# Value and gate projections in 512-column chunks through the two halves of `ogbuf`

## What is computed

```
mod = (silu(c) @ wmod) -> sa, ca, ga, sb, cb, gb
h = layernorm(x) * (1 + ca) + sa
q, k, v = h @ Wq.T, h @ Wk.T, h @ Wv.T          # 1024, 1024, 2048 wide; 4 heads
g = log_sigmoid(h @ Wgk1.T @ Wgk2.T + bgk2) / 32
o = gated linear attention(q, k, v, g)          # a recurrence over tokens
o = o * rsqrt(mean(o * o) + eps) * rms_w
x = x + ga * ((o * silu(h @ Wg.T)) @ Wout.T)    # gate 2048 wide
h = layernorm(x) * (1 + cb) + sb
x = x + gb * moe(h)                             # 8 experts, d_ffn 2048, top 2
```

## Time and profile before

| what | value |
|---|---|
| median of 3 runs | 3640.89 us |
| the profiled execution, its own time | 3633.7 us |
| its span on the slowest core (core 0) | 3632.2 us |
| spans of the 8 cores | 3603.2 to 3632.2 us |
| TensorE busy, share of the span | 2730.2 us, 75% |
| VectorE, ScalarE, GpSimd busy | 26%, 22%, 7% |
| share of the chain that ended last: TensorE, DMA | 64%, 9% |

### The profile page before, as it was taken

One profiled execution on the slowest core, in us unless ns is written; L12 is line 12 of the kernel. 1 busy time (PEld: TensorE's weight loads), 2 busy tenths in 40 slices (PEclk: granted clock), 3 DMA queues, 4 the chain that ended last, 5 costly groups with the idle time before them and its releaser, 6 DMA issues.

```text
span 3632.2 us, 37091 instructions; the slowest of 8 cores (3603.2 to 3632.2 us)
## 1 busy us (share of the span) xinstructions
PE 2730.2 (75%) x12923; PEld 1256.0 (35%) x12923; DVE 928.5 (26%) x1769; ACT 812.4 (22%) x1458; POOL 267.2 (7%) x463
## 2 busy tenths in 40 slices
PE   1474566467645755559999999999559999999997
PEld 0152225123411531114444444444124444444443
DVE  0323232333233223422112111212431111221221
ACT  0314231423342234211221112111321022111210
POOL 0010001001000100000100000000000010001000
PEclk9985678577757865669999999999679999999998
DMA  9361235034303520213543454434033344345334
GB/s 209 60 102 21 36 60 90 1 46 73 67 0 47 96 44 7 38 24 70 88 68 61 70 87 70 68 63 79 6 52 57 71 81 71 63 70 89 64 65 138
DMA packets 84362, 233.49 MB, mean 64 GB/s; under 512 B 7851, under 2 KB 8236, under 8 KB 82006
## 3 DMA queue, kind: packets, MB, share of 16 engines
q0 software_dynamic: 82400, 214.09, 35.4%
q1 hardware_dynamic: 1782, 17.03, 1.3%
HBM read 436.76 MB, written 8.39 MB: 123 GB/s over the span
## 4 chain that ended last, share of the span: by engine, by line
PE 64%; ACT 10%; DVE 9%; DMA 9%; issue 6%; DVEq 0%; ACTq 0%; POOL 0%; POOLq 0%
PE p L833 25%; PE p L804 22%; PE p L550 7%; PE p L675 3%; DMA vslab<-w1t 3%; DMA bigbuf<-wmod 3%; PE p L470 3%; DVE S L659 2%; ACT S_bf L663 2%; DMA ogbuf<-WgTt 1%; DMA ogbuf<-WvTt 1%; ACT bigbuf L606 1%; ACT scratch L629 1%; ACT scratch L621 1%; DVE scratch L451 1%
## 5 line engine op out<-in xcount | busy, mean ns | idle before, releaser
L804 PE MATMUL p<-hbuf,vslab 128*128 128x512 bf16 x4096 | 900.7, 381 | 19.9 <-DMA vslab<-w1t 14.5
L811 ACT ACTIVATE bigbuf<-p 128x512 bf16<-128x512 f32 x512 | 306.2, 598 | 1442.1 <-PE p L804 1401.8
L804 PEld LDWEIGHTS p<-hbuf,vslab 128*128 128x128 bf16 x4096 | 400.7, 98 | 515.6 <-issue 51.7
L833 PE MATMUL p<-bigbuf,wvg 128*128 128x512 bf16 x2048 | 460.6, 387 | 35.5 <-DVE bigbuf L816 35.5
L833 PE MATMUL p<-bigbuf,gslab 128*128 128x512 bf16 x2048 | 447.2, 379 | 0.0
L842 DVE SCALAR_TENSOR_TENSOR xTsb<-p,modc,xTsb 128x512 f32<-128x512 f32 x256 | 180.4, 746 | 743.8 <-PE p L833 743.8
L816 DVE TENSOR_TENSOR bigbuf<-bigbuf,vslab 128x1024 bf16<-128x1024 bf16 x256 | 177.3, 692 | 702.7 <-ACT bigbuf L811 701.0
L833 PEld LDWEIGHTS p<-bigbuf,wvg 128*128 128x128 bf16 x2048 | 202.6, 99 | 290.9 <-issue 60.6
L833 PEld LDWEIGHTS p<-bigbuf,gslab 128*128 128x128 bf16 x2048 | 200.4, 98 | 241.6
L550 PE MATMUL p<-ogbuf,hbuf 128*128 128x256 bf16 x1024 | 148.2, 315 | 111.0 <-DMA ogbuf<-WgTt 58.2
L794 POOL DMA_DIRECT2D vslab<-w1t x128 | 90.4, 708 | 1295.6 <-PE p L804 1253.6
(11 more groups left out here) (133 smaller groups left out, 1694.6 us busy)
## 6 DMA issues: line engine op xcount, KB each, us to landing
vslab<-w1t POOLq DMA_DIRECT2D x128, 512.0 KB, 6.3
wvg<-w2t POOLq DMA_DIRECT2D x64, 512.0 KB, 7.0
gslab<-w2t POOLq DMA_DIRECT2D x64, 512.0 KB, 9.1
hbuf<-WoutTt POOLq DMA_DIRECT2D x51, 256.0 KB, 5.2
bigbuf<-wmod POOLq DMA_DIRECT2D x8, 1536.0 KB, 16.7
wvg<-WvTt POOLq DMA_DIRECT2D x16, 512.0 KB, 9.2
ogbuf<-WvTt POOLq DMA_DIRECT2D x16, 512.0 KB, 5.7
wvg<-WgTt POOLq DMA_DIRECT2D x16, 512.0 KB, 9.5
```

What stands on the lines that cost most here:

```text
L804: T(lambda e, k=k, n2=n2, mi=mi, wb=wb, pbk=pbk: e.matmul(pbk[:, :], wb[:, mi * 1024 + k * 128: mi * 1024 + (k + 1) * 128], hbuf[:, k * 10 ...
L811: C(lambda e, m=m, n2=n2, pbk=pbk: e.activation(out=bigbuf[:, m * 1024 + n2 * 512: m * 1024 + (n2 + 1) * 512], in_=pbk[:, :], func=AF.Gelu ...
L833: T(lambda e, k=k, n2=n2, wb=wb, pbk=pbk: e.matmul(pbk[:, :], wb[:, k * 128:(k + 1) * 128], bigbuf[:, k * 1024 + n2 * 512: k * 1024 + n2 * ...
```

## The change

The chunks become 512 columns wide, 4 of `Wv` and 4 of `Wg` a slab. The pool of four is no longer used in this stage: chunk `nv` goes to half `nv % 2` of `ogbuf`, both halves under the one `Buf` `bogf`, and each chunk is loaded by two DMAs, which put their 256 columns beside each other in each of the 8 k-tiles. Matmuls, copies, Silu and products become 512 wide and half as many.

```diff
-            wvg_pool[0] = [wvg[:, 0:2048], wvg[:, 2048:4096],
-                           ogbuf[:, 0:2048], ogbuf[:, 2048:4096]]
-            bwvg_pool[0] = [bwvg[0], bwvg[1], bogf, bogf]
+            vg_bufs = [ogbuf[:, 0:4096], ogbuf[:, 4096:8192]]
...
-                for nv in range(8):
-                    wb, wbb = stream_wvg_chunk(wdram_, nv, 8, 256)
+                for nv in range(4):
+                    wb = vg_bufs[nv % 2]
+                    wbb = bogf
+                    for c_ in range(2):
+                        G(lambda e, nv=nv, c_=c_, wb=wb, wdram_=wdram_: e.dma_start(
+                            out=wb.rearrange("p (kt cm) -> p kt cm", kt=8)
+                            [:, :, c_ * 256:(c_ + 1) * 256],
+                            in_=wdram_[nv * 2 + c_]),
+                            writes=[wbb])
...
                             T(lambda e, k=k, t4=t4, wb=wb, pbk=pbk: e.matmul(
-                                pbk[:, 0:256],
+                                pbk[:, :],
...
-                                wb[:, k * 256:(k + 1) * 256],
+                                wb[:, k * 512:(k + 1) * 512],
...
-                                out=dstbuf[:, t4 * 2048 + nv * 256: t4 * 2048 + (nv + 1) * 256],
-                                in_=pbk[:, 0:256]),
+                                out=dstbuf[:, t4 * 2048 + nv * 512: t4 * 2048 + (nv + 1) * 512],
+                                in_=pbk[:, :]),
```

More of the change, by code:

```diff
@@ L563, in build_program @@
                               e.activation(
-                                  out=dstbuf[:, t4 * 2048 + nv * 256: t4 * 2048 + (nv + 1) * 256],
-                                  in_=pbk[:, 0:256], func=actf),
+                                  out=dstbuf[:, t4 * 2048 + nv * 512: t4 * 2048 + (nv + 1) * 512],
+                                  in_=pbk[:, :], func=actf),
                                 reads=[pbf], writes=[dstb])
                             V(lambda e, nv=nv, t4=t4, dstbuf=dstbuf: e.tensor_tensor(
[L568 to L571, removed]
+                                out=dstbuf[:, t4 * 2048 + nv * 512: t4 * 2048 + (nv + 1) * 512],
+                                in0=dstbuf[:, t4 * 2048 + nv * 512: t4 * 2048 + (nv + 1) * 512],
+                                in1=rmswbc[:, 0:512], op=ALU.mult),
                                 reads=[dstb, buf("rmswbc")], writes=[dstb])
```

## The result

The changed kernel takes 3962.75 us (median of 10 runs) against 3641.89 us: 1.0891 times the time of before, 95% interval 1.0874 to 1.0909. It is slower by 9%, inside the range of 3900 to 4440 us, but the forecast of 4144 us was for +510 us and the profiled execution shows +326 us (3960.01 against 3633.7). That is rival 1 of the prediction (3920 to 3999 us). Every kernel has some executions that are slower, with one half of the chip at a lower granted clock; the medians take them in and the ratios leave them out, so versions that lie close are compared by their ratios.

The account below looks back on a forecast made before the run. TensorE bounds the kernel, with waits on `ogbuf` loads in the v and g projections. Stage: 221 us matmuls + 608 + 53 for waits and half clock = 882 against 372, +510 on 3633.7, 4144 us; range 3900 to 4440.

Parts of the forecast that it names:

- rival 1: Loads into `ogbuf`: small runs cost little, 6.0 to 7.2 us from issue to continuation, time 3920 or 3999 us; chance 0.33.
- Direction and mechanism: v and g projections: slower by 510 us, as loads wait for TensorE's previous chunk and for each other under one name.
- The sum of one wait: Per chunk in v and g projections, TensorE stands 0.54 us to issue plus two 9.5 us load trips, 19.5 us.
- The hop: Time from a load's issue until the waiting engine goes on: 9.5 us, being 6.0 plus 3.5 for 896 more packets.
- the four rows for 128 more packets: From `w1t` loads: POOL's instruction +0.17 us, landing +0.9, issue-to-continuation +0.5, data start +0.5 or +1.5; each times 7.
- The first chunk of a slab: Loaded ahead in v and g projections, issued 7.8 us before TensorE is ready; waits 11 us, plus 2.2 at half clock.
- The half clock: Chunks behind a wait in v and g projections start at granted clock 0.50 and lose 2.2 us each.
- The matmuls: v and g projections: 32 chunks of 32 matmuls of 512 columns take 221 us against 223, gaining 2 us.
- VectorE and ScalarE at nothing: v and g projections: wider copies and products hidden under TensorE's matmuls, costed at nothing, between -0.5 and +0.5 us a slab.
- Rival 3: Loads into `ogbuf`: neither wait holds, the halves alternate, time about 3486 us; chance 0.03 together with its weaker form.
- its weaker form: Loads into `ogbuf`: only the wait for TensorE is void, 3682 us, about as before; chance within Rival 3's 0.03.

Follow-up runs that it names:

- e1_halves: The changed kernel with a separate name for each half of `ogbuf`; 3655.46 us, 1.0046 times before.
- e2_pair: The changed kernel with a name for each column half, shared by both halves of `ogbuf`; 3850.54 us, 1.0583 times before.
- e3_both: The changed kernel with four names, one for each half of `ogbuf` and column half; 3588.98 us, 0.9869 times before.
- e5_runs: The changed kernel with each load in one 4 KB run a partition, waits unchanged; median 4113.13 us of 4 runs, ratio 1.0760.
- e6_warm: The changed kernel with 56 useless filler matmuls ahead of every chunk but a slab's first; 3914.40 us, 1.0734 times before.
- e8_three: The changed kernel with `wvg` as third buffer beside both `ogbuf` halves, six names, 4 KB runs; 3523.92 us, 0.9674 times before.
- e4_before_names: The kernel before the change, with a separate name for each of the two `ogbuf` quarters; 3511.02 us, 0.9650 times before.
- e9_three_early: e8_three with the loads of a slab's first chunk issued ahead of the last four q and k weight loads; 3523.32 us, 0.9674 times before.
- e10_names_early: e4_before_names with its first two loads issued ahead of the last four q and k weight loads; 3545.04 us, 0.9715 times before.

## Why the prediction was right, and where its size was off

- *Direction and mechanism.* Right. TensorE waited 32 times for loads into `ogbuf`; POOL waited in turn for TensorE and for its own load. e1_halves and e2_pair take the two waits away one at a time, e3_both together, and the time falls by 307, 112 and 374 us.
- *The sum of one wait.* Right in form: 0.54 us from the last matmul to the issue, and two hops. The 28 waits behind the first are (397.7 - 26.9) / 28 = 13.2 us each, so a hop is 6.35 us.
- *The hop, the step that failed.* It was put at 9.5 us: 6.0 for the form of before and 3.5 for 896 more packets, from the `w1t` rows times 7. Measured are 6.35 us. By e5_runs the form of before takes (362.3 - 27.0) / 28 = 12.0 us a wait, a hop of 5.7, and the packets 0.6; so the 6.0 was near and the 3.5 failed. The fault was to put a difference between two kinds of load down to their packets, and to multiply it by 7. 56 x 3.15 + 4 x 4.3 = 194 us is the whole difference between the forecast +510 and the +318 of the stage. Of the four rows for 128 more packets the smallest, POOL's own instruction (+0.17 us, times 7 is 1.2), was the nearest, still twice too large: 710 - 536 ns for the first 128 more, but 873 - 528 for 896 more. The later landing, the longer hop and the later first packet of `w1t` are therefore not a matter of the number of packets. The 1024-packet load issued at 1054.25 us had its first packets 1.5 us later, sooner than `w1t` with its 256 (2.5 us). What `w1t`'s delay comes from was not tried. The rule of the Trainium skill, DMA: Bandwidth & Descriptors, that many descriptors can be emitted before the extra cost shows, is borne out: 0.6 us for 896. What the Trainium skill says in Perfetto Trace Analysis (the lifecycle of an instruction), that the profiled end of such a load is when its descriptors are made, fits as far as POOL's instruction grew by 0.35 us with the packets; where the other 0.25 us went no run shows.
- *The first chunk of a slab.* Put at 11 us, measured 6.1 to 7.7. The same hop is at fault. Only its first load took nearly as long as forecast (7.62 + 0.89 = 8.5 us at 1030 us, with the last q and k weights ahead of it in the queue), its second 5.9.
- *The half clock.* Put at 2.2 us a chunk, 32 times. The busy time gives (293.6 - 221) / 32 = 2.3, and e6_warm takes out 2.1 in each of the 23 chunks where its fillers leave at most 1.8 us idle. Right.
- *The matmuls.* 2 us of gain forecast; 6.91 against 6.98 us a pair in e8_three and e4_before_names. Right.
- *VectorE and ScalarE at nothing.* Right: they are busy 28 us of 172, and the profile shows no wait of the matmuls for them.
- *Rival 3,* the kernel without both waits, was put at 3486 us, and its weaker form, in which only the wait for TensorE is gone, at 3682; e1_halves, which is that form, took 3655, because hops of neighbouring chunks overlap. Four names on the changed kernel gave 3589 us, since two buffers leave each pair only one chunk to land under; the three buffers of e8_three gave 3524, the four narrow ones 3511. The expectations of e3_both, e4_before_names, e8_three, e9_three_early and e10_names_early were 15 to 50 us too low.

## What to carry to other kernels

Two buffers are only two if each has a name of its own in whatever tracks the dependences; look at the queue of the loads for a wait that ends with the matmuls of the chunk before, and count how often it stands. A load that is split into parts under one name pays a full trip for each part, some 6 us here for 512 KB, and smaller parts would save little: the 256 KB loads of the q and k weights landed in 5.0 to 5.3 us, these in 5.7. Wider matmuls were worth 1% of this stage, and names and depth of the buffers decided nearly all the rest: price the wait before the instruction.

## What the runs showed that was not expected

- 1024 packets of 512 B land nearly as fast as 128 of 4 KB: 5.7 us against 5.1 to 5.3 from issue to landing (the changed kernel and e5_runs).
- Serial waits cost less than they look when their names alternate: e1_halves keeps every pair in a row and is within 0.5% of the kernel before, which had waits of its own.
- A third level of the granted clock, neither 0.50 nor 1.00. In the first slab of e10_names_early, from 205 to 240 us, cores 2 and 3 ran their matmuls back to back at 0.81 while the other six ran at 1.00 (cores 1 and 2):

```profile
205.00:240.00 35.00, 35.00 (x323) 31.37 (x321) 15.16 (x39) 4.74 (x10) 5.29 (x10) 1.00 0.87 138
205.00:240.00 35.00, 35.00 (x269) 29.02 (x268) 13.46 (x32) 2.02 (x3) 4.23 (x8) 0.81 0.79 112
```

  Two 256-column chunks took 8.4 us there instead of 6.98. e8_three shows 0.81 on the same two cores (215 to 225 us), e9_three_early on cores 6 and 7, e4_before_names 1.00 on all eight. On core 2 of e10_names_early, its slowest, it cost 11 us: the chunks take 240.2 us against 228.9 on core 6. So a stage without waits may run into it, and it is a part of the miss of e9_three_early and e10_names_early; the 15 us of e4_before_names are not explained by it. What brings it on was not tried. The Trainium skill, TensorE: Matmul & The Clock Gate (Part 1), names a current limiter with a level of 13/16 for a whole die; the level agrees, but here only two of the die's four cores show it.
